# DVE instead of ACT writes the normalised rows of four layer norms in a transformer and Mamba kernel

## What is computed

```python
def _adaln(x, c, w, b):
    shift, scale, gate = jnp.split((c @ w + b)[:, None, :], 3, axis=-1)
    mu  = jnp.mean(x, axis=-1, keepdims=True)
    var = jnp.var(x, axis=-1, keepdims=True)
    return (x - mu) * jax.lax.rsqrt(var + EPS) * (1.0 + scale) + shift, gate

def step(hst, ins):                      # SSM: 512 channels, 64 states, 256 tokens
    dA  = jnp.exp(dt_t[:, :, None] * A)
    hst = hst * dA + (dt_t * x_t)[:, :, None] * B_t[:, None, :]
    return hst, jnp.einsum('bds,bs->bd', hst, C_t)

x = x + gt_a * attention(norm1(x));  x = x + gt_m * mlp(norm2(x))
x = x + gate * (ssm_forward(norm3(x)) + ssm_backward(norm3(x)))
x = x + gate * (silu(h @ w1) * (h @ w2)) @ w3         # h = norm4(x)
```

## Time and profile before

| | |
|---|---|
| median of 3 runs | 3376.75 us |
| the profiled execution, its own time | 3374.16 us |
| its span, first to last instruction | 3372.4 us |
| granted TensorE clock, mean | 0.971 |
| busy share of PE, DVE, ACT, POOL | 91%, 86%, 86%, 86% |
| the scans start | at about 194 us |
| one middle block, two passes | about 397 to 401 us |

### The profile page before, as it was taken

One profiled execution on the slowest core, in us unless ns is written; L12 is line 12 of the kernel. 1 busy time (PEld: TensorE's weight loads), 2 busy tenths in 40 slices (PEclk: granted clock), 3 DMA queues, 4 the chain that ended last, 5 costly groups with the idle time before them and its releaser, 6 DMA issues.

```text
span 3372.4 us, 72069 instructions
## 1 busy us (share of the span) xinstructions
PE 3081.1 (91%) x23032; PEld 2761.7 (82%) x23032; DVE 2909.0 (86%) x3331; ACT 2910.3 (86%) x6357; POOL 2906.0 (86%) x1552
## 2 busy tenths in 40 slices
PE   8789999999999999899999999899998999998877
PEld 6578888888888888888888888888988888888765
DVE  2269998899888998889988998889988899898985
ACT  1189999899988999889998898889998899999994
POOL 0069998899888998889988998889988899899995
PEclk6689999999999999999999999999999999999999
DMA  4011111111111111111111111111111111111111
GB/s 175 0 45 44 49 44 48 42 51 49 42 49 47 48 47 43 48 47 49 45 47 43 50 49 41 50 41 51 48 42 49 47 48 47 41 46 45 55 48 27
DMA packets 163040, 162.62 MB, mean 48 GB/s; under 512 B 17610, under 2 KB 156874, under 8 KB 162644
## 3 DMA queue, kind: packets, MB, share of 16 engines
q1 hardware_dynamic: 162644, 157.69, 16.9%
HBM read 154.44 MB, written 3.18 MB: 47 GB/s over the span
## 4 chain that ended last, share of the span: by engine, by line
PE 37%; POOL 27%; issue 23%; DVE 6%; ACT 5%; POOLq 1%; DVEq 0%; DMA 0%; ACTq 0%; SPq 0%
POOL hst L411 20%; PE ps L1258 9%; PE ps L1242 9%; POOL uBT L424 5%; PE ps L1005 5%; DVE hst L904 3%; ACT dA L579 3%; PE ps L1077 3%; PE ps L1014 2%; PE ps L1240 2%; PE ps L1052 2%; POOL uBT L421 2%; ACT uBT L565 1%; PE ps L1061 1%; PE ps L1250 1%
## 5 line engine op out<-in xcount | busy, mean ns | idle before, releaser
L411 POOL TENSOR_TENSOR hst<-hst,C_sb 128x1024 f32<-128x1024 f32 x1024 | 2443.3, 2407 | 237.8 <-DVE hst L904 233.3
L904 DVE TENSOR_TENSOR_SCAN hst<-dA,ps 128x512 f32<-128x512 f32 x2048 | 2382.6, 1204 | 162.3 <-PE ps L1258 141.1
L579 ACT ACTIVATE dA<-dt,A 128x255 f32<-128x255 f32 x4096 | 1749.5, 502 | 23.5 <-DVE hst L904 23.3
L1258 PE MATMUL ps<-ident,hst 128*128 128x128 f32 x8192 | 1242.9, 275 | 59.5 <-POOL hst L411 58.5
L1242 PE MATMUL ps<-ident,uBT 128*128 128x128 f32 x7104 | 1091.3, 277 | 40.5 <-DVE hst L904 32.1
L565 ACT ACTIVATE uBT<-uT,BT 128x512 f32<-128x512 f32 x1376 | 937.5, 718 | 138.1 <-PE ps L1242 95.9
L1258 PEld LDWEIGHTS ps<-ident,hst 128*128 128x128 f32 x8192 | 959.7, 141 | 83.6 <-POOL hst L411 80.8
L1242 PEld LDWEIGHTS ps<-ident,uBT 128*128 128x128 f32 x7104 | 846.1, 143 | 184.3 <-DVE hst L904 62.6
L424 POOL TENSOR_TENSOR uBT<-uT,BT 128x512 f32<-128x512 f32 x400 | 423.3, 1058 | 2.7 <-PE ps L1242 1.7
L1240 PE MATMUL ps<-uBT,uT 128*128 128x128 f32 x2176 | 299.1, 282 | 51.9 <-DVE hst L904 31.4
L1240 PEld LDWEIGHTS ps<-uBT,uT 128*128 128x128 f32 x2176 | 272.4, 195 | 65.7 <-DVE hst L904 39.4
(11 more groups left out here) (146 smaller groups left out, 2265.3 us busy)
## 6 DMA issues: line engine op xcount, KB each, us to landing
C_sb<-c_dram SPq DMA_DIRECT2D x1024, 128.0 KB, 2.9
gate_l<-gate_rows_dram SPq DMA_DIRECT2D x16, 256.0 KB, 3.6
x_att<-in_x_dram SPq DMA_DIRECT2D x8, 256.0 KB, 3.1
w<-in_L_cond_W_dram SPq DMA_DIRECT2D x2, 1024.0 KB
out_dram<-x_glu SPq DMA_DIRECT2D x8, 256.0 KB, 3.2
wg<-in_L_cond_mlp_w_dram SPq DMA_DIRECT2D x3, 512.0 KB, 11.4
w_xp<-_L_cond_fwd_xproj_w_dram SPq DMA_DIRECT2D x1, 1280.0 KB, 12.3
w_xp<-_L_cond_bwd_xproj_w_dram SPq DMA_DIRECT2D x1, 1280.0 KB, 14.9
```

The source lines that it names most:

```text
L411: pool.tensor_tensor(h, h, C_sb[:, n % FED:n % FED + 1, :].to_broadcast([P, KI, NB]), ALU.mult).then_inc(hC_ready.sem, 1)
L579: done = act.activation(dA[:, n % NT, c, lo:hi], dt[:, d, c, lo:hi], ACT.Exp, scale=A[:, d, c, n:n + 1])
L904: dve.tensor_tensor_scan(pair(hst[:, n % NR]), pair(dA[:, n % NT]), ps[:, BANK_U + (2 * n + e) % (2 * NU), :][:, way], 0.0, ALU.mult, ALU. ...
L1258: last = pe.matmul(ps[:, BANK_Y + j, c * P:(c + 1) * P], hst[:, n % NR, c, j * P:(j + 1) * P], ident[:, :], start=False, stop=(n == NS - 1 ...
```

## The change

The norm gets seven steps. ACT keeps the logarithm (step 2) and the exponential (step 3) and loses `neg_mean`, `offset` and `xn`. In the new step 4 DVE waits for `rstd` and makes `xn` by one instruction a row tile, `(x - mean) * rstd`, with mean and rstd as per-row operands. PE's transposes move to step 5, DVE's `hT` to step 6. The semaphores of `neg_mean` and `offset` go.

```diff
-    STEPS = dict(norm=6, ...)
-    ROOM = dict(norm=[HEAVY, LIGHT, HEAVY, HEAVY, LIGHT, LIGHT], ...
+    STEPS = dict(norm=7, ...)
+    ROOM = dict(norm=[HEAVY, LIGHT, HEAVY, LIGHT, HEAVY, LIGHT, LIGHT], ...
...
-  ... + meanwhile(stage("own", "dts", 2, 14), stage("last", "norm", 0, 4))
-      + meanwhile(stage("own", "dts", 14, 21), stage("last", "norm", 4, 6))
+  ... + meanwhile(stage("own", "dts", 2, 14), stage("last", "norm", 0, 5))
+      + meanwhile(stage("own", "dts", 14, 21), stage("last", "norm", 5, 7))
...
     # ACT, norm
                     if i == 2:
                         act.activation(rstd, mv[:, :, 1], ACT.Ln, bias=eps_col).then_inc(log_var[s].sem, 1)
-                        act.activation(neg_mean[:, :], mv[:, :, 0], ACT.Copy, scale=-1.0).then_inc(neg_ready[s].sem, 1)
                     if i == 3:
                         act.activation(rstd, rstd, ACT.Exp, scale=-0.5).then_inc(rstd_ready[s].sem, 1)
-                        for j in range(TT):
-                            last = act.activation(offset[:, j:j + 1], neg_mean[:, j:j + 1], ACT.Identity, scale=rstd[:, j:j + 1])
-                        ...
-                        for j in range(TT):
-                            last = act.activation(xn[:, j, :], x_of[:, j, :], ACT.Identity, bias=offset[:, j:j + 1], scale=rstd[:, j:j + 1])
-                        last.then_inc(xn_ready[s].sem, 1)
     # DVE, norm
-                    if i == 5:
+                    if i == 4:
+                        dve.wait_ge(rstd_ready[s].sem, rstd_ready[s].at(b, 1))
+                        for j in range(TT):
+                            last = dve.tensor_scalar(xn[:, j, :], x_of[:, j, :], mv[:, j, 0:1], rstd[:, j:j + 1], ALU.subtract, ALU.mult)
+                        last.then_inc(xn_ready[s].sem, 1)
+                    if i == 6:
     # PE, norm: the transposes
-                    if i == 4:
+                    if i == 5:
```

More of the change, by code:

```diff
@@ L59, in cond_transformer_mamba_kernel @@
     LIGHT, HEAVY, LONG, AMONG = 1.0, 2.0, 2.0, 1.0
-    STEPS = dict(norm=6, qkv=11, heads=37, proj=5, up=12, down=10, ins=12, dts=24, post=10, glu=17)
-    ROOM = dict(norm=[HEAVY, LIGHT, HEAVY, HEAVY, LIGHT, LIGHT], qkv=[HEAVY] * 10 + [LIGHT], heads=[LIGHT] * STEPS["heads"],
+    STEPS = dict(norm=7, qkv=11, heads=37, proj=5, up=12, down=10, ins=12, dts=24, post=10, glu=17)
+    ROOM = dict(norm=[HEAVY, LIGHT, HEAVY, LIGHT, HEAVY, LIGHT, LIGHT], qkv=[HEAVY] * 10 + [LIGHT], heads=[LIGHT] * STEPS["heads"],
                 proj=[LIGHT, HEAVY, HEAVY, LIGHT, HEAVY], up=[HEAVY] * 8 + [LIGHT, LIGHT, LONG, LIGHT], down=[HEAVY] * 8 + [LIGHT, HEAVY],
@@ L90, in order @@
             return (stage("own", "ins", 0, 10) + meanwhile(stage("last", "post"), stage("own", "ins", 10, 12))
-                    + stage("own", "dts", 0, 2) + meanwhile(stage("own", "dts", 2, 14), stage("last", "norm", 0, 4))
-                    + meanwhile(stage("own", "dts", 14, 21), stage("last", "norm", 4, 6))
+                    + stage("own", "dts", 0, 2) + meanwhile(stage("own", "dts", 2, 14), stage("last", "norm", 0, 5))
+                    + meanwhile(stage("own", "dts", 14, 21), stage("last", "norm", 5, 7))
                     + stage("own", "dts", 21, STEPS["dts"]) + stage("last", "glu") + first)
@@ L200, in cond_transformer_mamba_kernel @@
         rstd = sb("rstd", [P, TT])
-        neg_mean, offset = sb("neg_mean", [P, TT]), sb("offset", [P, TT])
         ones_col, eps_col = sb("ones_col", [P, 1]), sb("eps_col", [P, 1])
@@ L251, in cond_transformer_mamba_kernel @@
         att_mm, att_mods, wqk_ready, skip_ready = map(sem, ("att_mm", "att_mods", "wqk_ready", "skip_ready"))
-        offset_turns, hT_turns = sem("offset_turns"), sem("hT_turns")
+        hT_turns = sem("hT_turns")
         gate0_in, gate1_in = flow("gate0_in", 16), flow("gate1_in", 16)
@@ L257, in cond_transformer_mamba_kernel @@
         rstd_ready = [flow(f"rstd_ready{s}") for s in range(4)]
-        neg_ready = [flow(f"neg_ready{s}") for s in range(4)]
-        offset_ready = [flow(f"offset_ready{s}") for s in range(4)]
         xn_ready = [flow(f"xn_ready{s}") for s in range(4)]
@@ L459, in norm @@
                         act.activation(rstd[:, :], rstd[:, :], ACT.Exp, scale=-0.5).then_inc(rstd_ready[s].sem, 1)
-                        act.wait_ge(rstd_ready[s].sem, rstd_ready[s].at(b, 1))
-                        act.wait_ge(neg_ready[s].sem, neg_ready[s].at(b, 1))
-                        for j in range(TT):
-                            last = act.activation(offset[:, j:j + 1], neg_mean[:, j:j + 1], ACT.Identity, scale=rstd[:, j:j + 1])
-                        last.then_inc(offset_ready[s].sem, 1)
-                        act.wait_ge(offset_ready[s].sem, offset_ready[s].at(b, 1))
-                        act.sem_inc(offset_turns)
-                        x_of = (x_att, x_att, x_ssm, x_glu)[s]
-                        for j in range(TT):
-                            last = act.activation(xn[:, j, :], x_of[:, j, :], ACT.Identity, bias=offset[:, j:j + 1], scale=rstd[:, j:j + 1])
-                        last.then_inc(xn_ready[s].sem, 1)
                     yield
@@ L1301, in before @@
                             pe.wait_ge(o_raw.sem, o_raw.at(b + 1, H // 2))
-                        if plan.steps[j] == ("last", "norm", 4):
+                        if plan.steps[j] == ("last", "norm", 5):
                             pe.wait_ge(pre_ready.sem, pre_ready.at(p + 1, KI))
```

## The result

The changed kernel took 3465.48 us in the median (3461.49 to 3473.57, four runs), the kernel before 3376.43 in the same comparison: a ratio of 1.0268, 95% interval 1.0247 to 1.0288. That is 89 us slower. The forecast was 3440 with a range of 3400 to 3458: the direction was right, the size too small (66.6 us where 89 came), and the time lies 7.5 us above the range. The profiled execution took 3465.53, with a span of 3463.7 us and a mean granted TensorE clock of 0.962; before the span was 3372.4 and the clock 0.971.

What follows compares the result with a forecast made beforehand. At LN_ATT and LN_SSM the path was taken as DVE until hT, then PE. LN_ATT 6 x 4.4, LN_MLP 7 x 1.9, LN_SSM 7 x 3.1, LN_GLU 3, first forward LN_ATT 3.3, less 1.1: 66.6 us, so 3440; range 3400 to 3458.

Steps and rivals of the forecast that it cites:

- the pair: At each norm, DVE's two new instructions making xn: about 0.41 us for one alone, 0.75 us for both.
- LN_GLU: At LN_GLU, six alike: DVE's pair delays scan 41 and POOL, so L827 ends 0.5 us later each, 3 in all.
- moved steps of the backward passes: In backward passes, one slot more ahead of LN_SSM's products costs 1.1 us at each of 7; other moved steps about nothing.
- The turns: At the norms, DVE's new instructions and POOL's alternate by whole instructions; waits of 2.55 us in LN_ATT, 1.3 in LN_SSM.
- case A: At the norms, the pair's halves alternate with POOL's instructions: the forecast, 3440 us, own range 3422 to 3460, chance 0.40.
- Case B: At the norms, one wait only: the pair's second half starts before POOL gets its turn; 3418 us, chance 0.25.
- case C: At the norms, DVE's new instructions never wait for POOL; 3405 us, chance 0.15.
- D: At the norms, DVE's extra work lies in waits for PE and LN_GLU's 1.7 us come through; 3361 us, chance 0.09.
- E: Part of the delay is taken back in POOL's bound stretches and LN_GLU gives some; near 3374 us, chance 0.05.
- one slot more between statistics and hT is one less in `proj`, where DVE waits for PE: nothing: At LN_MLP, 7 norms: the longer norm's extra slot costs nothing; only pair and POOL waits count, 1.9 us each.
- about zero: In the backward pass, empty slot 16 is lost and one gained at the end, for no net cost.
- F: The moved steps meet POOL's turns worse than now; over 3458 us, chance 0.06.

Runs made afterwards that it cites:

- e10: e4 with the norm's third step at weight 1 in the plan of the backward passes only; 3398.85 us against 3380.79 for the kernel before.
- e1: The changed kernel's seven-step plan, but ACT still makes neg_mean, offset and xn as in the kernel before; 3405.08 us against 3378.58 before.
- e5: The changed kernel plus idle TensorE products while it waits for xn and hT at LN_ATT, LN_MLP and LN_SSM; 3447.46 us against 3373.85 before.
- e9: The changed kernel with the norm's third step at weight 1 instead of 2 in the backward passes only; 3452.98 us against 3380.79 before.
- e3: The changed kernel with one DVE instruction for both row tiles, using the first tile's mean and rstd; 3431.27 us against 3378.58 before.
- e4: The changed kernel, but in LN_ATT, LN_MLP and LN_SSM DVE's xn instruction takes rstd as a tensor from PSUM; 3426.85 us against 3378.58 before.
- e7: e1 with the norm's third step at weight 1 instead of 2 in forward and backward passes; 3395.98 us against 3373.85 before.

## Why the prediction was too small

| term | forecast | measured | from |
|---|---|---|---|
| the pair, the scan ahead of LN_ATT's products, LN_GLU, the edges: 20 x 0.75 + 0.75 + 6 x 1.1 + 3 - 1.1 | 24 | 23 | e10 |
| waits for POOL: 6 x 2.55 + 7 x 1.19 + 7 x 1.3 + 2.55 | 35 | 28 | L705's means in after |
| moved steps of the backward passes: 7 x 1.1 | 8 | 24 | e1 |
| TensorE's clock: 12 behind the norms, 5 in `proj` | none | 17 | e5, and the scans of after |
| sum | 67 | 92 | after: 91 |

That the sum closes to 1 us is in part luck: e9 shows that the terms don't add exactly, and the starts of passes, where the clock of before falls in 6, 10 and 12 too, move it by a few us either way.

Point by point:

- **The pair** was right: 0.40 to 0.41 us an instruction alone, 0.6 to 0.8 us a norm where nothing else is added (e10). So was the scan that the longer norm puts ahead of qkv, 1.1 us forecast and seen.
- **The turns** came as in case A at the sites looked at: 0.46 and 2.44 us for the two halves in LN_ATT, 0.47 and 1.12 in LN_MLP, 1.57 and 0.40 in LN_SSM. The sum was some 7 us too large, since a half overlaps with what it waits for and LN_MLP waited less than forecast. Case B and case C fall: e3 and e4, which make B and C true by force, are 34 and 39 us faster than after in the medians. The 39 are also more than the 28 that L705 waited.
- **LN_GLU** was right: from scan 36 to 49 the forward passes 2 to 12 of after lose 0.5 us each, 0.5 forecast. D, ACT's relief, is nowhere to be seen: no pass but the last forward one is shorter than before, and that by 2.0 us; and E, in which losses are taken back, falls with e1, whose backward passes lose more than forecast.
- **The step that failed first** is "one slot more between statistics and hT is one less in `proj`, where DVE waits for PE: nothing", and with it "about zero" for the moved steps of the backward pass. A slot less in a stage where DVE already waits is not free: the wait grows by the scan that no longer fills it, 1.01 to 2.24 us. And ACT's step 13 of `dts`, one slot earlier (the section on the change leaves it out of the steps that keep their slots), was not priced: 1.2 us a pass. e7 shows this by its backward passes, where the loss of e1 is gone to within 0.1 us a pass. F, the rival in which moved steps meet other work worse, had 0.06 and the wrong mechanism (POOL's turns); it is a quarter of the loss.
- **The step that was missing** is the clock. The prediction counted each stall of TensorE once, at its length. In six norms it cost 2.0 to 2.3 us more, behind the stall, where the products of the next stage ran at 1.2 GHz; two falls more in `proj` cost 2.5 each. The earlier trace rows shows why such a stage feels it: behind LN_ATT PE is busy 16.86 of 16.86 us, so slower products there have nothing to hide behind. That the clock would fall no row of before said: at these norms it stays at 1.00.
- **What would show it**: the scan behind LN_ATT's pair was to come 3.3 us later, and comes 2.7 later in the median, counted from the scan ahead of the norm; PE was to be idle 1.1 us longer ahead of the first qkv product, but that gap is 0.30, and the idle time stands one product earlier, 2.75 us ahead of the transposes; POOL's instruction was to be longer where it let DVE pass, and its pair took 4.73 for 4.69, so POOL's time doesn't show who waited.

Open: in which passes a stall of TensorE is followed by a fall. Ahead of LN_ATT's transposes after has 2.75 us in passes with a fall and 2.76 in pass 8 without one.

## What to carry to other kernels

A stall of TensorE just ahead of a stage that TensorE bounds is paid twice when the granted clock falls behind it: look up the clock in the stretch behind each stall that a change lengthens, price the next products at both speeds, and see whether the work behind them really comes later, since a fall that is over before the bound stage begins cost nothing here. A step more in a plan that spreads steps by weight moves the steps of other stages; keep the sum of weights and see which steps still move, or price each one, those in waits above all, since a wait that loses its filling grows. Two short DVE instructions that share something with POOL cost more than one of double length (34 us of 3465 here).
